# Softplus-squared attention: weights ringed by steps, squares of a step in one instruction, GpSimd's squares given to DVE and ScalarE

## What is computed

```
scores = einsum('bhqd,bhkd->bhqk', q, k) * hs ** (-0.5)
p = softplus(scores)
p = p * p
p = p * causal
attn = p / (sum(p, axis=-1) + 1e-09)
out = einsum('bhqk,bhkd->bhqd', attn, v)
```

## Time and profile before

| | us |
|---|---|
| three runs, median | 1626.35 |
| the profiled execution | 1625.58 |
| its span, first to last instruction | 1623.7 |
| of it the attention stage | 274 to 649 |

### The profile page before, as it was taken

How to read it: one execution, slowest core, us unless ns; L and a number is a source line. 1 busy time by engine, 2 the same in 40 slices (tenths; PEclk the granted TensorE clock), 3 DMA queues, 4 the chain that set the end, 5 groups by cost and what they waited for, 6 DMA issues and landing times. The chain is left out here.

```text
span 1623.7 us, 29032 instructions
## 1 busy us (share of the span) xinstructions
PE 1524.7 (94%) x11188; PEld 1122.8 (69%) x11188; DVE 1247.4 (77%) x2386; ACT 853.9 (53%) x1356; POOL 694.7 (43%) x478
## 2 busy tenths in 40 slices
PE   8999888899999897999999999988999999799998
PEld 7888776444444443988877787766777777678787
DVE  5554896999999999565568888767877777677886
ACT  3333487777777785433333222258888887421210
POOL 0002112999999998400234222112655555211111
PEclk9999999999999999999999999999999999999999
DMA  4000166667756770000010000012333332100000
GB/s 160 21 1 14 35 193 168 100 88 97 101 78 93 97 103 4 10 5 1 13 40 20 1 1 1 1 55 80 105 106 105 105 106 105 40 14 26 14 26 27
DMA packets 57017, 95.80 MB, mean 59 GB/s; under 512 B 7760, under 2 KB 29488, under 8 KB 56880
## 3 DMA queue, kind: packets, MB, share of 16 engines
q1 hardware_dynamic: 55920, 93.35, 26.1%
q10 hardware_dynamic: 960, 0.59, 0.1%
HBM read 76.88 MB, written 17.04 MB: 58 GB/s over the span
## 5 line engine op out<-in xcount | busy, mean ns | idle before, releaser
L1429 DVE TENSOR_TENSOR att_weights<-att_weights 128x1024 f32<-128x1024 f32 x144 | 320.2, 2246 | 11.3 <-ACT att_weights L1403 11.3
L1492 POOL TENSOR_TENSOR att_weights<-att_weights 128x1024 f32<-128x1024 f32 x112 | 314.8, 2843 | 4.8 <-ACT att_weights L1403 3.4
L1403 ACT ACTIVATE att_weights<-ps 128x1024 f32<-128x1024 f32 (+1 forms) x288 | 268.1, 976 | 81.6 <-PE ps L1345 50.9
L927 DVE SCALAR_TENSOR_TENSOR X<-ps,moe_gsel,X 128x256 f32<-128x256 f32 x512 | 246.0, 483 | 72.7 <-PE ps L48 50.6
L48 PE MATMUL ps<-w_experts_hi,moe_xh 128*128 128x512 f32 x512 | 204.0, 399 | 0.0
L48 PE MATMUL ps<-w_experts_hi,moe_xl 128*128 128x512 f32 x512 | 203.2, 397 | 0.0
L48 PE MATMUL ps<-w_experts_lo,moe_xh 128*128 128x512 f32 x512 | 201.5, 393 | 0.0
L1363 PE MATMUL ps<-att_weights,att_v_ones 64*32 64x64 f32 (+5 forms) x2048 | 159.8, 401 | 29.6 <-DVE v L1450 15.6
L424 ACT ACTIVATE ffn_gates<-ps,ffn_gate_bias 128x512 f32<-128x512 f32 x72 | 49.6, 689 | 148.2 <-PE ps L48 128.7
L1363 PEld LDWEIGHTS ps<-att_weights,att_v_ones 128*32 128x32 f32 (+1 forms) x2048 | 53.4, 108 | 97.6 <-issue 49.3
L996 POOL TENSOR_TENSOR X<-X,moe_bias_sb 128x512 f32<-128x512 f32 x32 | 41.4, 1294 | 184.9 <-DVE X L927 162.3
(11 more groups left out here) (282 smaller groups left out, 3679.8 us busy)
## 6 DMA issues: line engine op xcount, KB each, us to landing
ssm_lb<-decays SPq DMA_DIRECT2D x32, 512.0 KB, 4.7
ssm_rise<-decays SPq DMA_DIRECT2D x28, 512.0 KB, 3.8
qk_parts<-qkv_part SPq DMA_DIRECT2D x32, 384.0 KB, 2.8
q_stack<-qk_parts SPq DMA_DIRECT2D x64, 128.0 KB, 4.9
k_stack<-qk_parts SPq DMA_DIRECT2D x64, 128.0 KB, 8.3
att_q_stack<-qk_parts SPq DMA_DIRECT2D x64, 128.0 KB, 4.9
att_k_stack<-qk_parts SPq DMA_DIRECT2D x64, 128.0 KB, 8.7
out<-X SPq DMA_DIRECT2D x7, 512.0 KB, 2.9
```

The costliest lines, as they stand in the source:

```text
L927: dve.scalar_tensor_tensor(out=x, in0=ring[:, e // 2, (e % 2) * C:(e % 2 + 1) * C], scalar=gsel[:, s, j, e:e + 1], in1=x, op0=ALU.mult, op ...
L1403: act.activation(Wt[:, u % WU, 0:n], scores(u)[:, 0:n], ACT.Softplus).then_inc(plus_done, 1)
L1429: dve.tensor_tensor(wt, wt, wt, ALU.mult).then_inc(sq_dve, 1)
L1492: pool.tensor_tensor(wt, wt, wt, ALU.mult).then_inc(sq_pool, 1)
```

## The change

The ring `att_weights` is laid out by steps: 6 places (`WS`) of two units each, as many bytes as before; an upper step takes a place for itself and uses a quarter of it. The softplus of a unit in step m waits for the value step m - 6. A square now takes a whole step in one instruction, 2048 elements per partition (512 for the upper steps). DVE squares steps 0, 1, 3, 4, 6, 7 and 8 of a pass, once the second unit of the step has its softplus; ScalarE squares steps 2, 5 and 9 (`ACT_STEPS`), each after the softplus of the next step's first unit; GpSimd squares none and keeps its two copies. A value step waits for one semaphore.

```diff
-    SU, WU = 3, 12
-    assert NU % SU == 0 and NU % WU == 0
-
-    BY_DVE, BY_POOL, BY_ACT = range(3)
-    engine_of = [BY_ACT if BANKS[u % PU] == 1 else BY_POOL if u % PU in (1, 3, 6, 8, 10, 13, 15) else BY_DVE for u in range(NU)]
+    SU, WS = 3, 6
+    assert NU % SU == 0
+
+    step_begin = [0] + [end + 1 for end in step_end[:-1]]
+    BY_DVE, BY_ACT = range(2)
+    ACT_STEPS = (2, 5, 9)
+    engine_of = [BY_ACT if m % PS in ACT_STEPS else BY_DVE for m in range(NS)]
...
-        Wt = sb("weights", [P, WU, 2, BANK], F32)
+        Wt = sb("weights", [P, WS, 2, 2, BANK], F32)
...
+        def weights_of(i, m):
+            wide = BANKS[step_end[m] % PU]
+            return Wt[:, (i * NS + m) % WS, 0:step_end[m] + 1 - step_begin[m], 0:wide]
...
-                for u in range(base + products[0][2], base + last + 1):
-                    pe.wait_ge(squared[engine_of[u]], i * squares[engine_of[u]][NU] + squares[engine_of[u]][u + 1])
+                made = squares[engine_of[m]]
+                pe.wait_ge(squared[engine_of[m]], i * made[NS] + made[m + 1])
...
-                before = step_of[u - WU] + NS if u >= WU else step_of[u - WU + NU]
-                act.wait_ge(pv_done, i * NS + before + 1)
-                n = BANKS[u % PU]
-                act.activation(Wt[:, u % WU, 0:n], scores(u)[:, 0:n], ACT.Softplus).then_inc(plus_done, 1)
+                m, n = step_of[u], BANKS[u % PU]
+                if i * NS + m >= WS:
+                    act.wait_ge(pv_done, NS + i * NS + m - WS + 1)
+                act.activation(weights_of(i, m)[:, u - step_begin[m]], scores(u)[:, 0:n], ACT.Softplus).then_inc(plus_done, 1)
...
-                    if u and engine_of[u - 1] == BY_ACT:
-                        square(i, u - 1)
+                    m = step_of[u] - 1
+                    if u == step_begin[m + 1] and m >= 0 and engine_of[m] == BY_ACT:
+                        square(i, m)
...
-            def square(i, u):
-
-                dve.wait_ge(plus_done, SU + i * NU + u + 1)
-                wt = Wt[:, u % WU, 0:BANKS[u % PU]]
+            def square(i, m):
+
+                dve.wait_ge(plus_done, SU + i * NU + step_end[m] + 1)
+                wt = weights_of(i, m)
                 dve.tensor_tensor(wt, wt, wt, ALU.mult).then_inc(sq_dve, 1)
...
-                    if engine_of[u] == BY_DVE:
-                        square(i, u)
+                    if u == step_end[step_of[u]] and engine_of[step_of[u]] == BY_DVE:
+                        square(i, step_of[u])
...
-                    if engine_of[u] == BY_POOL:
-                        pool.wait_ge(plus_done, SU + i * NU + u + 1)
-                        wt = Wt[:, u % WU, 0:BANKS[u % PU]]
-                        pool.tensor_tensor(wt, wt, wt, ALU.mult).then_inc(sq_pool, 1)
```

More of the change, by code:

```diff
@@ L1283, in attention_phase @@
     TURN_LAG, COPY_LAG, DEN_LAG, OUT_LAG = 4, 7, 9, 10
-    SU, WU = 3, 12
-    assert NU % SU == 0 and NU % WU == 0
-    BY_DVE, BY_POOL, BY_ACT = range(3)
-    engine_of = [BY_ACT if BANKS[u % PU] == 1 else BY_POOL if u % PU in (1, 3, 6, 8, 10, 13, 15) else BY_DVE for u in range(NU)]
-    squares = [[sum(engine_of[x] == e for x in range(u)) for u in range(NU + 1)] for e in range(3)]
+    SU, WS = 3, 6
[4 more added lines that the diff above has]
+    engine_of = [BY_ACT if m % PS in ACT_STEPS else BY_DVE for m in range(NS)]
+    squares = [[sum(engine_of[x] == e for x in range(m)) for m in range(NS + 1)] for e in range(2)]
     def outputs_at(x, ends, n, lag, i, first, stage):
@@ L1320, in attention_phase @@
         s_done, plus_done, pv_done = sem("s_done"), sem("plus_done"), sem("pv_done")
-        sq_dve, sq_pool, sq_act = squared = sem("sq_dve"), sem("sq_pool"), sem("sq_act")
+        sq_dve, sq_act = squared = sem("sq_dve"), sem("sq_act")
+        def weights_of(i, m):
+            wide = BANKS[step_end[m] % PU]
+            return Wt[:, (i * NS + m) % WS, 0:step_end[m] + 1 - step_begin[m], 0:wide]
         oT_done, o_turned, den_done, rec_done, o_done = (sem(n) for n in ("oT_done", "o_turned", "den_done", "rec_done", "o_done"))
@@ L1349, in value_step @@
                 s, (qb, last, products) = m // PS, pass_steps[m % PS]
-                base = s * PU
                 if m % PS == 0:
@@ L1363, in value_step @@
                     ins = pe.matmul(O(qb)[h * 2 * HD:(h + 1) * 2 * HD, q0:q0 + w], values,
-                                    Wt[rows, (base + unit) % WU, t, c:c + w], start=kj == 0 and part == FULL, stop=part == UPPER and kj == (qb + 1) * GT - 1)
+                                    Wt[rows, (i * NS + m) % WS, s * PU + unit - step_begin[m], t, c:c + w], start=kj == 0 and part == FULL, stop=part == UPPER and kj == (qb + 1) * GT - 1)
                 ins.then_inc(pv_done, 1)
@@ L1375, in body @@
                 for m in range(NS):
-                    begin, end = step_end[m - 1] + 1 if m else 0, step_end[m] + 1
+                    begin, end = step_begin[m], step_end[m] + 1
                     for u in range(begin, end):
@@ L1408, in _ @@
             act.sem_inc(plus_done, SU)
-            def square(i, u):
-                act.wait_ge(plus_done, SU + i * NU + u + 1)
-                wt = Wt[:, u % WU, 0:BANKS[u % PU]]
+            def square(i, m):
+                act.wait_ge(plus_done, SU + i * NU + step_end[m] + 1)
+                wt = weights_of(i, m)
                 act.activation(wt, wt, ACT.Square).then_inc(sq_act, 1)
@@ L1417, in _, with square @@
                     softplus(i, u)
-                    if u and engine_of[u - 1] == BY_ACT:
-                        square(i, u - 1)
-                if engine_of[NU - 1] == BY_ACT:
-                    square(i, NU - 1)
+                    m = step_of[u] - 1
+                    if u == step_begin[m + 1] and m >= 0 and engine_of[m] == BY_ACT:
+                        square(i, m)
+                if engine_of[NS - 1] == BY_ACT:
+                    square(i, NS - 1)
         @block.vector
         def _(dve):
-            def square(i, u):
-                dve.wait_ge(plus_done, SU + i * NU + u + 1)
-                wt = Wt[:, u % WU, 0:BANKS[u % PU]]
+            def square(i, m):
+                dve.wait_ge(plus_done, SU + i * NU + step_end[m] + 1)
+                wt = weights_of(i, m)
                 dve.tensor_tensor(wt, wt, wt, ALU.mult).then_inc(sq_dve, 1)
```

## The result

The changed kernel takes 1601.25 us (median of 4, 1599.91 to 1601.98) against 1625.74 for the kernel before (4 runs): ratio 0.9844, 95% interval 0.9829 to 0.9858, 24.5 us less. The profiled execution took 1601.98 us, its span is 1600.1. The forecast was 1601, 25.3 us less.

The account below looks back on a forecast made before the run. GpSimd was taken to bound the attention stage at 23.08 us per pass; after the change, TensorE's 20.9 plus a 0.6 wait makes 21.5, saving 1.58 in 16 passes, 25.3 us: 1626.35 to 1601 us, range 1589 to 1615.

Parts of the forecast that it names:

- Turns at one port: DVE's and GpSimd's SBUF squares never overlap; two units cost one turn of each, about 2.87 us.
- DVE's wide square: DVE's joint square of 2048 elements, seven per pass, takes 2.2 us each, 15.4 us in all.
- ScalarE's long square: The added 2048 square of step 5 on ScalarE, once per pass: 1.91 us alone, 1.8 chained.
- TensorE's work: TensorE's unchanged matmuls take 20.8 to 21.0 us per pass, making it next late after GpSimd.
- The wait at unit 15: TensorE's scores of unit 15 wait behind ScalarE's long square: 4.47 - 3.87 = 0.6 us per pass.
- The output chain: DVE's work up to the divide takes 6.3 us; TensorE needs it for value step 3 at 6.99, so it fits.
- GpSimd's copies: GpSimd's two copies of v per pass may take the port during DVE's output chain: about 0.5 us, hidden by room.
- The sum: New pass 20.9 + 0.6 = 21.5 us, 1.58 saved in each of 16 passes, 25.3 us: 1601 us.
- Rival 1: No bubble: TensorE runs through at 20.8 us per pass, kernel 1590 us; chance 0.13.
- Rival 3: GpSimd only along for the ride: score, softplus and value step loop takes 23 us itself, 1626 us; chance 0.05.
- Rivals 2 and 4: Output chain sets pace, TensorE waits 1.4 us, 1614 us, chance 0.17; wide DVE square misses short rate, 1660 us, chance 0.04.
- The signs: Expected trace: DVE squares 2.15 to 2.4 us, GpSimd under 60 us, copies 21.5 apart, TensorE busy over 95% of stage.

Follow-up runs that it names:

- e11: Kernel before with the divide right behind the reciprocal in DVE's queue (lag 9 in place of 10): 1627.90 us, ratio 1.0011.
- e4: Changed kernel plus seven idle GpSimd products per pass on a spare 128x768 tile, which nobody reads or waits for: 1664.25 us in one run.
- e6: Changed kernel with the square of step 5 on GpSimd (one instruction of 2048) in place of ScalarE: 1590.91 us in one run.
- e2: Changed kernel with step 5 squared by DVE too, ScalarE squaring the upper steps alone: 1587.15 us, ratio 0.9766 to the kernel before.
- e1: Changed kernel with ScalarE's joint square of step 5 split into two instructions of 1024: 1593.42 us, ratio 0.9791 to the kernel before.
- e5: Changed kernel with an idle ScalarE square of a spare 128x768 tile ahead of the step 5 square, once per pass: 1612.37 us in one run.
- e7: Changed kernel with the divide three units later in DVE's queue (lag 13 in place of 10): 1688.17 us in one run.
- e9: Kernel before, ring by units kept, with all seven GpSimd squares per pass given to DVE unit by unit: 1591.41 us, ratio 0.9801.
- e8: Kernel before with one of GpSimd's seven squares per pass (unit 13) given to DVE: 1631.29 us, ratio 1.0036.
- e3: Changed kernel with DVE's squares unit by unit, 14 of 1024 per pass instead of 7 of 2048: 1598.75 us, ratio 0.9831 to the kernel before.

## Why the prediction was right

- **The stage and its pace.** GpSimd was named as the one that sets the pace. Of the kernel before that is true as far as it goes: no gap in its row, 3.4 us of waits. But e11 and the later passes of the kernel before show DVE's queue at the same 23 us, stretched by the same turns, and the prediction treated DVE as a sufferer with no limit of its own. The change relieves both, so the number didn't suffer.
- **Turns at one port.** Right: in e4 products on a tile of their own lengthen DVE's squares; e6 shows one turn at its place.
- **DVE's wide square.** 2.2 taken, 2.15 to 2.32 as bounds, 2.28 at the median, of which some 0.08 lies under the next instruction.
- **ScalarE's long square.** 1.91 and 1.8 in a chain; measured 1.90, and 396.14 to 397.94 is 1.80.
- **TensorE's work.** 20.8 to 21.0; e2 shows 20.69 without waits, so 20.9 was 0.2 too much.
- **The wait at unit 15.** 0.6 forecast, 0.50 measured in nearly every pass, by the chain that was named (e1, e5). From the start of unit 11's scores (394.58) ScalarE's chain took 4.43 to the scores of unit 15, and TensorE was there after 3.93; 4.47 and 3.87 were forecast.
- **The output chain.** It fits, as said: no wait for the divide is left in the trace after. e7 gives the laid-out pass its test: 4.81 where 4.8 was worked out.
- **GpSimd's copies.** 0.5 us was assumed; a DVE square beside one is 2.41 in place of 2.28 (0.13).
- **The sum.** 21.5 per pass against a mean of 21.49. The undisturbed pass is 21.35, 20.7 + 0.5 and some 0.15 that no run explains; a few longer passes (one of 22.76 above all) make up the rest. So two small errors of the forecast, TensorE's work and the wait, each 0.1 to 0.2 too high, met irregular passes that it didn't have. That the two means agree to 0.01 us is luck. The mean before, 23.08, has an irregular pass in it as well (24.91).
- **The rivals.** Rival 1 (no wait) is what e1 and e2 make: 1593 and 1587. Rival 3 (a loop of 23 us without GpSimd) falls with e9, where GpSimd has no square and the pass is 20.7, though e8 looks like it. Rivals 2 and 4 did not occur. Rival 2's wait is 8.3 - 6.99 = 1.3, not 1.4, which moves its time by under 2 us.
- **The signs.** All but one are met: TensorE is busy 329.28 of 350 us, 94.1% of the stage, where over 95% was asked; from 325 to 601 it is 95.3%.

The rule that smaller instructions may help where an engine causes bubbles ("Perfetto Trace Analysis" of the Trainium skill, "Optimizing Scalar/DVE Operations") was weighed with 10 us left in the kernel; e1 splits the one square and gains 8 us. The run agrees with it, on ScalarE. On DVE the split (e3) changes nothing, since nobody waits for those squares.

## What to carry to other kernels

When two engines take turns at a port, look at both of their queues with the other's turns inside: taking one piece of work from the busier of them can leave the time no better (e8), while taking all of it can pay at once (e9). A joint instruction should be charged to whoever waits for what is queued behind it: the same joining cost 0.5 us per pass on ScalarE and nothing on DVE. And before crediting a change of several parts, run its parts: here one line of the old kernel gave more than the whole.

## What the runs showed of the hardware

A wait of 4 to 4.8 us on TensorE was followed by the lower clock: in e7 the value step behind it took 1.94 us in place of 1.07, and the mean granted clock was 0.89. The idle stretch of 1.88 us in e1 was followed by it too (0.50 from 376 to 378 us). Waits of 0.5 to 1.2 us (the change, e5) left it at 1.00 in the steady stretch. So a long wait costs more than its length: in e7 a pass takes about 27.4 us, where 21.35 - 0.5 + 4.81 = 25.7 would be the wait alone, some 1.7 us less.

DVE's squares and GpSimd's products lengthened each other on tiles that have nothing in common (e4: 2.28 to 3.01 us and 1.47 to 3.33), while DVE's copy from PSUM kept its 0.68 us beside a GpSimd square (e6).

GpSimd's small copy of v, 0.40 us when DVE leaves the port free, takes 2.34 beside 2048 squares, as if it had to sit one out; nobody waits for it in the steady stretch, so this costs nothing here.
